# A mixture-of-experts layer: ten dense experts against two dense experts and 15 blocks of routed rows

## The reference, cut to what matters

```
def _expert(xf, w1, w3, w2):
    return jax.nn.silu(xf @ w1) * (xf @ w3) @ w2        # w1, w3: 512 x 256, w2: 256 x 512
...
logits = xf @ router_w + router_b                       # 8 routed experts
topk_vals, topk_idx = jax.lax.top_k(logits, 2)
gates = softmax of the two chosen logits, 0 elsewhere
routed = jax.vmap(_expert, in_axes=(None, 0, 0, 0))(xf, routed_w1, routed_w3, routed_w2)
routed_out = jnp.einsum('etd,te->td', routed, gates)
shared_out = ...(xf, shared_w1, shared_w3, shared_w2).sum(axis=0)   # 2 shared experts, gate 1
x = x + routed_out + shared_out                         # xf is the layer norm of x
```

## Time and profile before

| | us |
|---|---|
| median of 3 runs | 3105.52 |
| fastest and slowest run | 3099.84, 3106.57 |
| profiled execution, first to last instruction | 3110.7 |
| TensorE busy in it | 2897.3 (93%) |
| VectorE, ScalarE, GpSimd busy | 1610.5, 1191.9, 83.5 |
| mean granted TensorE clock | 0.970 |
| experts_stage | about 551 to 904.6 |

### The profile page before, as it was taken

One profiled execution on the slowest core, in us unless ns is written; L12 is line 12 of the kernel. 1 busy time (PEld: TensorE's weight loads), 2 busy tenths in 40 slices (PEclk: granted clock), 3 DMA queues, 4 the chain that ended last, 5 costly groups with the idle time before them and its releaser, 6 DMA issues. The chain is left out here.

```text
span 3110.7 us, 55469 instructions
## 1 busy us (share of the span) xinstructions
PE 2897.3 (93%) x23641; PEld 2302.6 (74%) x23644; DVE 1610.5 (52%) x3377; ACT 1191.9 (38%) x1885; POOL 83.5 (3%) x67
## 2 busy tenths in 40 slices
PE   6998998999989999999999999999999976479987
PEld 3444777788877888888888888888888865467864
DVE  4333525454454555455555554555555462774487
ACT  2212222332343444334443344433444330535675
POOL 0000101000000000000000000000000013001000
PEclk9999999999999999999999999999999988789988
DMA  7987010111211111101111011110111019305310
GB/s 260 316 291 255 2 44 25 41 54 47 81 52 49 46 47 38 41 14 46 46 38 41 15 46 46 33 41 20 46 47 36 29 59 134 73 29 167 115 21 28
DMA packets 174040, 222.36 MB, mean 71 GB/s; under 512 B 56416, under 2 KB 109664, under 8 KB 173424
## 3 DMA queue, kind: packets, MB, share of 16 engines
q1 hardware_dynamic: 144336, 197.75, 20.3%
q10 hardware_dynamic: 29472, 21.24, 3.4%
HBM read 206.36 MB, written 10.49 MB: 70 GB/s over the span
## 5 line engine op out<-in xcount | busy, mean ns | idle before, releaser
L91 PE MATMUL xa_J<-xa_c_hi,xa_wk_hi 128*128 128x402 f32 x1024 | 365.0, 356 | 4.7 <-ACT xa_kT L1973 3.4
L2085 DVE CUSTOM_DVE_ANT_0 xa_pr<-xa_S,xa_m 128x402 f32<-128x402 f32 x512 | 270.9, 571 | 166.0 <-PE xa_S L2234 166.0
L92 PE MATMUL xa_J<-xa_c_lo,xa_wk_hi 128*128 128x402 f32 x1024 | 354.7, 346 | 0.0
L93 PE MATMUL xa_J<-xa_c_hi,xa_wk_lo 128*128 128x402 f32 x1024 | 354.6, 346 | 0.0
L91 PE MATMUL xa_J<-xa_wv_hi,xa_c_hi 128*128 128x512 f32 (+1 forms) x832 | 335.3, 403 | 0.0
L1973 ACT ACTIVATE xa_kT<-xa_J,cl_bk 128x402 f32<-128x402 f32 x256 | 151.8, 593 | 458.8 <-PE xa_J L93 458.8
L93 PE MATMUL xa_J<-xa_wv_hi,xa_c_lo 128*128 128x512 f32 (+1 forms) x832 | 327.3, 393 | 0.0
L92 PE MATMUL xa_J<-xa_wv_lo,xa_c_hi 128*128 128x512 f32 (+1 forms) x832 | 327.3, 393 | 0.0
L2112 DVE TENSOR_TENSOR cl_v<-xa_J,cl_bv 128x512 f32<-128x512 f32 (+1 forms) x208 | 143.5, 690 | 263.4 <-PE xa_J L93 225.7
L1989 ACT ACTIVATE xa_pr<-xa_pr,xa_nm 128x1608 f32<-128x1608 f32 x128 | 208.6, 1632 | 95.0 <-DVE xa_nm L2101 95.0
L91 PEld LDWEIGHTS xa_J<-xa_c_hi,xa_wk_hi 128*128 128x128 f32 x1024 | 193.1, 189 | 66.6 <-ACT xa_kT L1973 43.3
(11 more groups left out here) (468 smaller groups left out, 5469.9 us busy)
## 6 DMA issues: line engine op xcount, KB each, us to landing
bl_rows<-in_ctx SPq DMA_DIRECT2D x40, 1024.0 KB, 8.7
main_x<-in_ctx_cols SPq DMA_DIRECT2D x192, 201.0 KB, 2.9
bl_cols<-in_ctx_cols SPq DMA_DIRECT2D x24, 1024.0 KB, 10.7
main_qoT<-in_L_ffn_w ACTq DMA_DIRECT2D x32, 512.0 KB, 3.8
main_x<-in_ctx_cols SPq DMA_DIRECT2D x64, 197.5 KB, 2.6
moe_raw<-in_L_ffn_routed_w SPq DMA_DIRECT2D x24, 512.0 KB, 4.0
main_qoT<-in_L_attn_W SPq DMA_DIRECT2D x16, 512.0 KB, 3.7
bl_early<-in_ctx SPq DMA_DIRECT2D x8, 768.0 KB, 12.7
```

The source lines that it names most:

```text
L91: pe.matmul(out, w_hi, x_hi, start=first, stop=False)
L92: pe.matmul(out, w_hi, x_lo, start=False, stop=False)
L93: return pe.matmul(out, w_lo, x_hi, start=False, stop=last)
L2085: nc.vector.tensor_tensor_reduce(out=pr[:, r, ks], in0=S[:, r, 0:KG], in1=m[:, ks], scale=1.0, scalar=NEVER, op0=ALU.add, op1=ALU.max, acc ...
```

## The change

The eight routed experts are no longer applied to every token. Expert number 0 and 1 of the stage are now the two shared ones, dense as before and with a plain add. While they run, the router's result is turned into places: every (token, choice) pair gets a slot in a DRAM buffer `routed_in` of 15 x 256 rows, the pairs of one expert next to each other and padded to whole blocks of 256 (`rank` on TensorE counts with 16 small products, `allot` on VectorE works out `slot`, and `owner`, the expert of each block). SP fills the buffer with zeros (7.86 MB). GpSimd writes the normed rows to their slots with 16 indirect DMAs of 128 rows, 256 KB each. Then all engines run 15 blocks: SP loads the block's rows and the weights of its owner (read from SBUF into a register), TensorE turns the rows with 8 transposes, `block_hidden` makes 48 products of 256 columns and `block_out` 12 of 512, and SP stores the 256 result rows to `routed_out`. The split w1 and w3 have two buffers now (`weights_of`), raw13, raw2 and the split w2 still one. At the end GpSimd fetches the rows of each pair with 16 indirect DMAs into a ring of seven, and VectorE adds them with their gates (`combine`, `finish`). SP loads Wq, Wk and Wv behind the last store. All 15 blocks run, whatever the router chose; the work space is lent from cl_v, qoT and the buffers of the next stage's queries. `load13`, `load2`, `block_silu`, `block_gated` and the like follow the pattern of the functions before. `choose` has four more small steps, `weigh` loses its loop of 16 and the table of gates.

```
+BLOCK = 2 * P
+BLOCKS = (TILES * P * 2 + EXPERTS * (BLOCK - 1)) // BLOCK
+SLOTS = BLOCKS * BLOCK
+RING = 7
...
+    def __init__(self, nc, cross, qoT):
+        self.sent = nc.dram_tensor("routed_in", (SLOTS, D), F32, kind="Internal").ap()
+        self.made = nc.dram_tensor("routed_out", (SLOTS, D), F32, kind="Internal").ap()
+        self.results = room[:, 0:4 * D].rearrange("p (b i d) -> p b i d", b=2, i=2)
+        self.tokens = cross.v[:, 0:TILES, :]
+        self.blocks = cross.v[:, TILES:TILES + 4, :].rearrange("p (b i) d -> p b i d", b=2)
+        self.back = [room[:, (4 + i) * D:(5 + i) * D] for i in range(4)] + [cross.v[:, TILES + 4 + i, :] for i in range(RING - 4)]
+        self.x_hi, self.x_lo = cross.a_hi.halves[0], cross.a_lo.halves[0]
+        self.w13 = [h[:].rearrange("p k n -> p (k n)").rearrange("p (j k h) -> p j k h", j=2, k=KC) for h in (cross.wq_hi, cross.wq_lo)]
...
+        def weights_of(n):
+            return w13[0 if n < 2 else (n - 1) % 2]
+        def columns(j):
+            return slice((j % 2) * BLOCK, (j % 2 + 1) * BLOCK)
...
+                nc.gpsimd.memset(rows.zero, 0.0).then_inc(zero_ready, 1)
...
+                pool.wait_ge(zero_stored, 16)
+                pool.wait_ge(norm.normed, TILES)
+                pool.wait_ge(rows_ready, 4)
+                pool.wait_ge(slot_ready, 1)
+                for c in range(2):
+                    for t in range(TILES):
+                        i = c * TILES + t
+                        nc.gpsimd.indirect_dma_start(out=rows.sent, out_offset=bass.IndirectOffsetOnAxis(ap=slot[:, i:i + 1], axis=0),
+                                                     in_=rows.tokens[:, t, :], in_offset=None).then_inc(sent, 16)
+                for i in range(2):
+                    pool.wait_ge(b_stored[i], 16 * len(range(i, BLOCKS, 2)))
+                for n in range(PAIRS):
+                    t, c = n // 2, n % 2
+                    if n >= RING:
+                        pool.wait_ge(combined, n - RING + 1)
+                    i = c * TILES + t
+                    nc.gpsimd.indirect_dma_start(out=rows.back[n % RING], out_offset=None, in_=rows.made,
+                                                 in_offset=bass.IndirectOffsetOnAxis(ap=slot[:, i:i + 1], axis=0)).then_inc(back[n % RING], 16)
...
+                def load13(n, e, w1, w3):
+                    sp.wait_ge(w13_lo_ready, 4 * n)
+                    sp.dma_start(raw13[:, 0, :, :], w1[e].rearrange("(k p) h -> p k h", p=P)).then_inc(w13_loaded, 16)
+                    sp.dma_start(raw13[:, 1, :, :], w3[e].rearrange("(k p) h -> p k h", p=P)).then_inc(w13_loaded, 16)
+                def load2(n, e, w2):
+                    sp.wait_ge(w2_lo_ready, n)
+                    sp.dma_start(raw2[:], w2[e].rearrange("(k p) n -> p k n", p=P)).then_inc(w2_loaded, 16)
...
+                def first_weights(j):
+                    load13(2 + j, owner_of(j), routed[0], routed[1])
...
+                def load_block(j):
+                    if j >= 2:
+                        sp.wait_ge(b_turned, j - 1)
+                    sp.dma_start(rows.blocks[:, j % 2], rows.rows_of_block(rows.sent, j)).then_inc(b_loaded[j % 2], 16)
+                def store_block(j):
+                    sp.wait_ge(kept_act, j + 1)
+                    sp.wait_ge(kept_dve, j + 1)
+                    sp.dma_start(rows.rows_of_block(rows.made, j), rows.results[:, j % 2]).then_inc(b_stored[j % 2], 16)
+                sp.wait_ge(zero_ready, 1)
+                sp.dma_start(rows.cleared(), rows.zero[:, None, :].to_broadcast([P, BLOCKS, 2 * D])).then_inc(zero_stored, 16)
+                load13(1, 1, shared[0], shared[1])
+                load2(1, 1, shared[2])
+                sp.wait_ge(owner_ready, 1)
+                first_weights(0)
+                sp.wait_ge(sent, 16 * PAIRS)
+                load_block(0)
+                load_block(1)
+                second_weights(0)
+                first_weights(1)
+                for j in range(BLOCKS):
+                    if j + 2 < BLOCKS:
+                        load_block(j + 2)
+                    if j:
+                        second_weights(j)
+                    if j >= 2:
+                        store_block(j - 2)
+                    if j + 2 < BLOCKS:
+                        first_weights(j + 2)
+                store_block(BLOCKS - 2)
+                store_block(BLOCKS - 1)
+                sp.wait_ge(b_turned, BLOCKS)
                 cross.load_weights(sp)
...
                 def split13(n):
+                    j = n - 2
                     act.wait_ge(w13_loaded, 32 * n + 32)
+                    if j >= 2:
+                        act.wait_ge(b_produced, j - 1)
+                    for i in range(2):
+                        split_hi(nc, weights_of(n)[0][:, i], raw13[:, i]).then_inc(w13_hi_ready, 1)
 
...
+                def keep_row(t):
+                    nc.scalar.activation(rows.tokens[:, t, :], x_sb[:, t, :], ACT.Identity, bias=norm.shift[:, t:t + 1],
+                                         scale=norm.rstd[:, 0, t:t + 1]).then_inc(rows_ready, 1)
+                def block_high(j):
+                    act.wait_ge(b_turned, j + 1)
+                    if j >= 2:
+                        act.wait_ge(b_produced, j - 1)
+                    split_hi(nc, rows.x_hi[:, :, columns(j)], front).then_inc(b_hi_ready, 1)
...
+                def block_h_high(j):
+                    act.wait_ge(b_h32, j + 1)
+                    if j >= 2:
+                        act.wait_ge(b_out, 2 * (j - 1))
+                    split_hi(nc, h_hi[:, :, columns(j)], flat(h32, j)).then_inc(b_h_hi, 1)
...
+                block_high(0)
+                for j in range(BLOCKS):
+                    if j + 1 < BLOCKS:
+                        block_high(j + 1)
+                    if j + 1 < BLOCKS:
+                        split13(3 + j)
+                    block_silu(j)
+                    block_h_high(j)
+                    if j:
+                        keep_block(j - 1)
+                        split2(2 + j)
+                keep_block(BLOCKS - 1)
                 cross.query_high(act)
...
+                def allot():
+                    dve.wait_ge(ranked, 1)
+                    nc.vector.tensor_copy(ranks[:], O[:, 0, 64:64 + (TILES + 1) * EXPERTS]).then_inc(ranks_kept, 1)
...
+                def combine(n):
+                    t, c = n // 2, n % 2
+                    dve.wait_ge(back[n % RING], 16 * (n // RING + 1))
+                    if c:
+                        dve.wait_ge(combined, n)
+                    nc.vector.scalar_tensor_tensor(out=x_sb[:, t, :], in0=rows.back[n % RING], scalar=gain[:, c, t:t + 1],
+                                                   in1=x_sb[:, t, :], op0=ALU.mult, op1=ALU.add).then_inc(combined, 1)
+                def finish(t):
+                    combine(2 * t)
+                    combine(2 * t + 1)
+                    dve.wait_ge(combined, 2 * t + 2)
+                    feeds.gather(dve, t)
...
+                block_low(0)
+                for j in range(BLOCKS):
+                    if j + 1 < BLOCKS:
+                        block_low(j + 1)
+                    if j + 1 < BLOCKS:
+                        for i in range(4):
+                            split13(3 + j, i)
+                    block_gated(j)
+                    block_h_low(j)
+                    if j:
+                        keep_block(j - 1)
+                        split2(2 + j)
+                keep_block(BLOCKS - 1)
                 cross.query_low(dve)
-                gated(LAST, 0)
-                gated(LAST, 1)
-                low(LAST, 0)
-                low(LAST, 1)
-                dve.wait_ge(gate_ready, N)
                 for t in range(4):
                     finish(t)
                 feeds.invert(dve, 0)
-                gated(LAST, 2)
+                finish(4)
+                finish(5)
                 feeds.low(dve, 0)
                 feeds.low(dve, 1)
-                low(LAST, 2)
-                gated(LAST, 3)
-                low(LAST, 3)
+                finish(6)
                 feeds.low(dve, 2)
+                finish(7)
                 feeds.low(dve, 3)
...
+                def rank():
...
+                def turn_block(j):
+                    pe.wait_ge(b_loaded[j % 2], 16 * (j // 2 + 1))
+                    if j == 0:
+                        pe.wait_ge(added, 2 * TILES)
+                    else:
+                        pe.wait_ge(b_lo_ready, j)
+                    for k in range(KC):
+                        for i in range(2):
+                            last = pe.transpose(front[:, k, i * P:(i + 1) * P], rows.blocks[:, j % 2, i, k * P:(k + 1) * P], ident[:])
+                    last.then_inc(b_turned, 1)
+                def block_hidden(j):
+                    pe.wait_ge(b_lo_ready, j + 1)
+                    pe.wait_ge(w13_lo_ready, 4 * (2 + j) + 4)
+                    hi, lo = weights_of(2 + j)
```

(39 more changed lines are left out.)

331 lines of the change are left out of this document (192 added, 139 removed).

## The result

The changed kernel takes 3024.49 us (median of four runs, 3019.74 to 3030.77) against 3106.05: 0.9735 of the time before, 95% interval 0.9714 to 0.9755, 81.6 us less. The forecast was 3025.0. A second set of five runs gave the same ratio of 0.9735. The profiled execution took 3019.74 us and spans 3018.0, 92.7 under the one of before; 11 us of that is luck of the two executions: this one was 4.7 under its median, and the one of before, whose time I put at its span and the 1.7 us that a time lies over its span, some 6.4 over.

The account below looks back on a forecast made before the run. TensorE's products were taken as the bound. From the second expert's first product to the next stage, terms summed to 224.7 us instead of 305.1, 80.4 less, giving 3025 us; range 3006 to 3068.

Parts of the forecast that it names:

- bridge: Between expert 1 and hidden(0): last add, turn, high, low and turn again, 5.1 us together.
- up to out(13): Blocks after hidden(0): turn and hidden(1) 6.8 us, then 13 beats of 9.7, 126.1 us.
- The products: TensorE in the blocks: 0.122 us per 256-column product, 0.227 per 512-column one, 9.7 us a block.
- Slack 0.8: Raw13's single-buffer loop of load and splits: 8.9 us a block, under TensorE's beat of 9.7 by 0.8.
- rival B: Raw13's loop sets the block beat: 11.2 us if other traffic delays the weight pair, +21, 3046 us; chance 0.20.
- Rival A: Weight loads pace TensorE's 256-column products at 0.19 us: 3.3 more a block, +49, 3074 us; chance 0.12.
- Rival C: Weight loads don't overlap TensorE's products at all: 9 us more a block, +136, 3161 us; chance 0.01.
- The price of an indirect DMA: POOL's scatters and gathers: 1.4 us each, the geometric mean of 0.77 and 2.6.
- Rival D: POOL's indirect DMAs at both ends of the blocks cancel the gain at 4.5 us each; 3137 at 5.5; chance 0.03.
- The front: Before expert 1: ranking, allotting, fill and scatters cost nothing; expert 1 starts as before, 0, between -3.6 and +3 us.
- The tail: After the last block product: VectorE's chain of query_low, combines, statistics, inversion and lows ends at E + 35.1 us.
- pj_out's start: Next stage's first products after the tail: TensorE idles through the tail, so they start at half clock, as before.

Follow-up runs that it names:

- e2: Changed kernel with one more 1 MB load per block, read by nobody: 3034.90 us profiled.
- e1: Changed kernel with the third product of every triple in block_hidden left out, 32 products a block instead of 48: 3023.49 us profiled.
- e6: Changed kernel with a second raw buffer for w1 and w3 of every other block: 3018.38 us profiled.
- e7: Changed kernel with a second raw w1/w3 buffer and the third product of every block_hidden triple left out: 3008.08 us profiled.
- e5: Changed kernel with block_hidden's 48 products over only the first 128 of 256 columns: 3026.68 us profiled.
- t1: Changed kernel with query_low moved behind tile 0's combines in the tail: 3022.19 us profiled.
- e3: Changed kernel with the zero fill issued twice and GpSimd waiting for both before the scatters: 3023.76 us profiled.
- e4: Changed kernel with each of the 16 scatters issued twice and SP waiting for all 32: 3033.26 us profiled.
- t2: Changed kernel with the loads of Wq, Wk and Wv moved out of the tail to earlier places: median 3020.63 us, ratio 0.9711.

## Why the prediction was right, step by step

The whole: forecast -80.5, measured -81.6 in the medians. In the profiles -92.7: 1.7 ahead of the stage's first product, 86.8 up to the last product into xa_J (the stage itself is 87.7 shorter), 4.2 behind, in stages that the change doesn't touch. That the two agree to 1 us is partly luck: the stretch came out 6.5 us shorter than its sum, and the front and the other stages moved by several us between executions. Of the sum for the stretch, term by term:

| term | taken | measured |
|---|---|---|
| expert 1 | 32.7 | 34.2 |
| bridge | 5.1 | 5.4 |
| hidden(0) | 8.9 | 7.3 |
| up to out(13) | 132.9 | 128.2 |
| out(13), wait, out(14) | 9.7 | 8.7 |
| tail | 35.4 | 34.4 |
| sum | 224.7 | 218.2 |

- **The products** were right: 0.118 for 0.122. The beat was 0.35 too long: the turn took 0.79 for 0.88, the hidden products 5.74 or 5.84 for 5.86 and the output ones 2.76 for 2.72, and the 0.2 for changes of shape is already in these. The sum also counted one turn too many (0.9), block 14 having none ahead of it. Expert 1 has a wait of 1.1 us at 609.23: ScalarE's first silu came 8.2 us behind its table load instead of 3.1 in the second profile, which hasn't this wait; what held the silu isn't shown.
- **"Slack 0.8" of raw13's loop was wrong, and is the weak step.** I took 5.1 from issue to landing and 8.9 in all; it is 5.4 to 6.2 and 9.2 to 10.1, likely because block rows and results share the engines (e2's extra 1 MB a block made the rounds 10.4). So rival B's mechanism is there, at a seventh of its size: the loop is 9.6 and not 11.2, 0.2 us a block over TensorE's beat and not 1.5. Even that did not show, because the lead of the first blocks, which the forecast never mentions, lasted for 10 to 13 beats. With more blocks each further one would have taken 9.6. That the loop stands there is shown by e1, e6 and e7; that the forecast held in spite of it is luck in part, since TensorE's beat taken, 9.7, happened to cover the loop's too.
- **Rival A** (a load sets the pace) fell as stated, 0.12 and not 0.19 apart, but e5 shows a floor of 0.11: my argument from two loads 0.11 apart may have read the floor itself. **Rival C** (no overlap) fell: records of 0.19 us of load inside steps of 0.12. The rule that the Trainium skill gives in "TensorE: Matmul & The Clock Gate" (The mechanism, the heading in front of the one that the prediction names), overlap only between different row groups, isn't what these full-height products do.
- **The price of an indirect DMA** was 1.4 taken, 1.26 measured on GpSimd (0.96 busy and 0.30 to the next). From issue to landing a scatter took 2.7 us at the least and a gather 3.5 to 6.5 (t1), but several are in flight at once, so it isn't paid 16 times. **Rival D** fell with it. The 2.6 us, an estimate by the Trainium skill's figures ("DMA: Bandwidth & Descriptors", Anatomy of one DMA), is close to the 2.7 of a scatter: it is a length, and the prediction tried it as a pace.
- **The front** held: the first scatter started at 587.5 for 588.5 taken, expert 1 0.8 us earlier counted from the router's first product (the range's ends worked out there, 597.0 and 600, are -2.5 and +0.5, and not the -3.6 and +3 that it states), scatters over at 608, fill landed 22.5 us after its issue (23 to 26 taken). "Nothing" for the fill and the scatters agrees with the trace, and e3 and e4 show where it ends.
- **The tail** was right in sum and partly by luck: I had query_low end at E + 13.5 (11.5 it was) and 21.6 us behind it (22.5). That the gathered rows would land only with it, 6.6 us behind their issue in t1 beside the weight loads and 3.4 in t2 without them, was not in either chain.

```profile
790.05 2.29 DVE L106 TENSOR_TENSOR crossq_wq_lo<-cl_v,crossq_wq_hi 128x2048 fp32r<-128x2048 f32 x1 [9.75 <-ACT crossq_wq_hi L102]
792.26 1.61 DVE L1820 SCALAR_TENSOR_TENSOR main_x<-main_qoT,ex_gain,main_x 128x512 f32<-128x512 f32 x2
...
814.19 0.67 DVE L106 TENSOR_TENSOR crossq_a_lo<-ex_O,crossq_a_hi 128x512 fp32r<-128x512 f32 x1
```

(VectorE in the tail of the changed kernel: query_low, the first combines, the last low half.)

- **pj_out's start** "at half clock, as it did": it did, but for 5.7 us instead of 3.1 behind the product of the earlier trace rows, some 1.3 us more.

## What to carry to other kernels

When every wait hides behind one busy engine, compare the period of each closed loop with that engine's beat, not its waits: a loop that is 2.5% slower and started with a lead shows nothing until the lead is gone, and any later saving on the busy engine is lost to it. Before saving TensorE time here, give raw13 a second buffer; the DMA engines at 0.92 are the next place to look. What you put in front of a loop or a queue that is as slow as you are comes back as a wait.

## What the runs showed of the hardware

- A DMA issue can hold SP. Behind the 7.86 MB fill the next three 512 KB issues took 7.9, 5.1 and 6.8 us instead of 0.4; in e3, with two fills, one took 19.1. SP's queue in order of time:

```profile
551.22 0.65 SPq L1563 DMA_DIRECT2D routed_in<-main_qoT  x1
551.93 7.87 SPq L1536 DMA_DIRECT2D moe_raw<-in_L_ffn_shared_w  x1
559.84 5.10 SPq L1537 DMA_DIRECT2D moe_raw<-in_L_ffn_shared_w  x1
564.98 6.75 SPq L1541 DMA_DIRECT2D moe_raw<-in_L_ffn_shared_w  x1
```

- Products of 128 columns start no closer than 0.111 us, of 256 columns 0.118; at half clock both 0.213. Over products of 128 columns in e5 the granted clock stayed at 0.50 from 640.5 to 664.4, with TensorE without a gap, while over 256 columns in the changed kernel it was at 0.50 from 636.8 to 640.2 only.
- Whether the clock falls over one idle stretch varies from run to run: after the same wait of 2.94 us the twelve products of out(14) started within 2.6 us in one profile of the changed kernel, at full clock throughout, and within 4.2 in the other, where it was at 0.50 from 780.1 to 783.6.
- The DMA engines gave 352 GB/s at a share of 0.99 in e2 with this mix of weights, rows and results.
